# Causal masks of the score blocks: from an added product on TensorE to the reduction on VectorE, and finer waits around scores, V products and maxima

## The reference

```python
x = x + xattn(layernorm(x), ctx, ctx, Wq, Wk, Wv, bv, Wo, bo)
x = x + ffn(layernorm(x), fast_b, w_fc, w_proj, u, v, gate)

# xattn: 16 heads of 32
scores = einsum('bhsd,bhtd->bhst', qh, kh) * scale
mask = triu(ones((Sq, Sq), dtype=bool), k=0).at[0, 0].set(False)
scores = where(mask, -inf, scores)
probs = softmax(scores, axis=-1)
out = einsum('bhst,bhtd->bhsd', probs, vh)

# ffn: both weights rounded to -1, 0, 1 times a row's scale
h = bitlinear(x, w_fc) + gate * (x @ v.T @ fast_b.T @ u.T)
r = maximum(h, 0)
return bitlinear(r * r, w_proj)
```

## Time and profile before

| | |
|---|---|
| median of three executions | 2602.8 us |
| the profiled execution | 2611.11 us |
| its span, first to last instruction | 2609.3 us |
| attention phase, set-up and 16 batches | to about 1565 us |
| TensorE busy | 2522.3 us, 97% |
| VectorE busy | 1763.4 us, 68% |
| ScalarE busy | 1021.1 us, 39% |
| GpSimd busy | 789.4 us, 30% (all in the attention phase) |
| mean granted TensorE clock | 0.992 |

### The profile page before, as it was taken

One profiled execution on the slowest core, in us unless ns is written; L12 is line 12 of the kernel. 1 busy time (PEld: TensorE's weight loads), 2 busy tenths in 40 slices (PEclk: granted clock), 3 DMA queues, 4 the chain that ended last, 5 costly groups with the idle time before them and its releaser, 6 DMA issues. The chain is left out here.

```text
span 2609.3 us, 45260 instructions
## 1 busy us (share of the span) xinstructions
PE 2522.3 (97%) x13762; PEld 1908.1 (73%) x13762; DVE 1763.4 (68%) x3748; ACT 1021.1 (39%) x1887; POOL 789.4 (30%) x1498
## 2 busy tenths in 40 slices
PE   6999999999999999999999989999999999999998
PEld 5676677677667667667667758888888888888887
DVE  5676776776776677677677665666666666666663
ACT  3433533433433443353343344333333333333332
POOL 1743643654564473474365350000000000000000
PEclk9999999999999999999999999999999999999999
DMA  4444354354354344445435341111111111111111
GB/s 150 114 125 128 95 143 131 77 156 119 88 146 132 88 127 133 115 108 133 135 84 154 117 130 37 48 48 48 48 48 48 48 48 48 48 48 48 48 52 46
DMA packets 147811, 240.79 MB, mean 92 GB/s; under 512 B 26419, under 2 KB 34611, under 8 KB 147780
## 3 DMA queue, kind: packets, MB, share of 16 engines
q1 hardware_dynamic: 143684, 239.35, 32.1%
q10 hardware_dynamic: 4096, 1.06, 0.2%
HBM read 100.85 MB, written 37.77 MB: 53 GB/s over the span
## 5 line engine op out<-in xcount | busy, mean ns | idle before, releaser
L845 ACT ACTIVATE probs<-bank 128x512 f32<-128x512 f32 x640 | 358.4, 597 | 287.9 <-PE bank L633 278.7
L1243 PE MATMUL h_bank<-xT_hi,wT 128*128 128x512 f32 x1024 | 398.4, 389 | 0.5 <-ACT projT L1274 0.5
L1244 PE MATMUL h_bank<-xT_lo,wT 128*128 128x512 f32 x1024 | 398.3, 389 | 0.0
L1258 PE MATMUL y_bank<-projT,wT 128*128 128x512 f32 x1024 | 398.3, 389 | 0.0
L1260 PE MATMUL y_bank<-projT,wT 128*128 128x512 f32 x1024 | 398.3, 389 | 0.0
L1310 ACT ACTIVATE acc<-h_bank,scale_fc 128x512 f32<-128x512 f32 x256 | 176.4, 689 | 487.4 <-PE h_bank L1247 487.4
L532 POOL TENSOR_SCALAR_AFFINE_SELECT probs<-probs 128x256 f32<-128x256 f32 (+1 forms) x640 | 229.1, 372 | 212.0 <-ACT probs L845 204.1
L608 PE MATMUL bank<-stack 96*128 96x512 f32 (+3 forms) x1024 | 263.0, 337 | 21.5 <-DMA stack<-stage 15.1
L937 DVE CUSTOM_DVE_ANT_0 bank<-bank,masks 128x512 f32<-128x512 f32 x256 | 178.3, 696 | 141.1 <-PE bank L608 132.9
L633 PE MATMUL bank<-stack 98*128 98x512 f32 (+3 forms) x1024 | 259.1, 337 | 11.6 <-DMA stack<-m_stage 8.7
L1386 DVE CAST wT<-acc 128x512 fp32r<-128x512 f32 x256 | 108.4, 423 | 214.2 <-ACT acc L1315 214.2
(11 more groups left out here) (173 smaller groups left out, 4641.4 us busy)
## 6 DMA issues: line engine op xcount, KB each, us to landing
stack<-stage SPq DMA_DIRECT2D x768, 128.0 KB, 2.3
xc_rows<-in_x_dram SPq DMA_DIRECT2D x16, 1024.0 KB, 5.3
x_res<-in_x_dram SPq DMA_DIRECT2D x16, 1024.0 KB, 6.0
x<-x_res SPq DMA_DIRECT2D x64, 256.0 KB, 2.3
xc_rows<-x SPq DMA_DIRECT2D x16, 1024.0 KB, 5.6
x_res<-x SPq DMA_DIRECT2D x16, 1024.0 KB, 7.7
out_dram<-y_sb SPq DMA_DIRECT2D x64, 256.0 KB, 2.0
xc_rows<-in_ctx_dram SPq DMA_DIRECT2D x15, 1024.0 KB, 5.3
```

What stands on the lines that cost most here:

```text
L845: act.activation(probs[:, s[2], :], t_bank[u % 2][:, :], ACT.Exp, scale=SCALE).then_inc(exp_done, 1)
L1243: pe.matmul(h_bank[b % 2][:, :], fcT[:, k, cols], xT_hi[:, k, :], start=k == 0, stop=False)
L1244: pe.matmul(h_bank[b % 2][:, :], fcT[:, k, cols], xT_lo[:, k, :], start=False, stop=False)
L1258: pe.matmul(y_bank[j][:, :], a_hi[:, b % RING, P * j:P * j + P], projT[:, b, :], start=b == 0, stop=False)
```

## The change

- All masks are added by VectorE. The mask products of line 612 go. For units 1 and 3 VectorE issues two `tensor_tensor_reduce` of 384 and 128 columns, for unit 4 two of 256, where it had two plain reductions or one. Each is followed by its accumulator read. All units now have their wait alone in front.
- Each head has a `qk_stacked` semaphore of its own. S waits at k = 0 for the three copies of the pair's first head, at k = 2 for those of the second. ScalarE waits for all heads before it overwrites `stage`.
- PV of row block 0 waits for 8 selected units, of row block 1 for 9, of row block 2 for 10.
- SEND issues the copy of the rounded maxima behind `m_hi`, and waits for `m_free` only ahead of the second copy.

```diff
-        qk_stacked = [[sem(f"qk_stacked{s}{p}") for p in range(2)] for s in range(2)]
+        qk_stacked = [[sem(f"qk_stacked{s}{h}") for h in range(GH)] for s in range(2)]
...
+        mask_row = masks[:, :, :].rearrange("p m x -> p (m x)")
...
-                                     ).then_inc(qk_stacked[g % 2][pair], 16)
+                                     ).then_inc(qk_stacked[g % 2][h], 16)
...
                 if u < 4:
                     block(2 * pair + u // 2, 2, 384, 0)
-                    block(2 * pair + u // 2, 0, 128, 384, start=False)
-                    return mask(out[:, 256:512], masks[:, 3:5, :].rearrange("p m x -> p (m x)"))
+                    return block(2 * pair + u // 2, 0, 128, 384, start=False, stop=True)
                 block(2 * pair, 1, 256, 0)
-                block(2 * pair + 1, 1, 256, 256, start=False)
-                return mask(out[:, :].rearrange("p (h t) -> p h t", h=2)[:, :, P:2 * P],
-                            masks[:, 3:4, :].broadcast_to([P, 2, P]))
+                return block(2 * pair + 1, 1, 256, 256, start=False, stop=True)
...
-                        if s[2] in (0, 5):
-                            pe.wait_ge(qk_stacked[s[1] % 2][s[2] // 5], (i * 2 + s[1] // 2 + 1) * 96)
+                        if s[2] % 5 in (0, 2):
+                            pe.wait_ge(qk_stacked[s[1] % 2][2 * (s[2] // 5) + s[2] % 5 // 2], (i * 2 + s[1] // 2 + 1) * 48)
...
+                        if r != 3:
+                            pe.wait_ge(selected, i * TB + UNITS * g + {0: 8, 1: 9, 2: 10}[r])
                         if r == PV_ORDER[0]:
-                            pe.wait_ge(selected, i * TB + UNITS * g + UNITS)
...
-                        wait_alone(act, act_passed, (m_free, i * GROUPS + s[1] + 1))
-                        for part in range(2):
+                        for part, (written, value) in enumerate(((m_hi, i * GROUPS + s[1] + 1),
+                                                                 (m_free, i * GROUPS + s[1] + 1))):
+                            wait_alone(act, act_passed, (written, value))
                             act.dma_start(stack[s[1] % 2][96 + part:97 + part, 0, :, :].bitcast(F32)
...
-                            for p in range(2):
-                                staged(act, [q[p] for q in qk_stacked], s[1], b, 96)
+                            for h in range(GH):
+                                staged(act, [q[h] for q in qk_stacked], s[1], b, 48)
...
+                        wait_alone(dve, dve_passed, (s_full, i * SB + u + 1))
+
+                        def largest(first, behind, mask_from, col):
+                            return dve.tensor_tensor_reduce(bank_u[:, first:behind], bank_u[:, first:behind],
+                                                            mask_row[:, mask_from:mask_from + behind - first], 1.0, LOWEST,
+                                                            ALU.add, ALU.max, maxima[:, col:col + 1])
+
                         if k < 4 and k % 2 == 0:
-                            wait_alone(dve, dve_passed, (s_full, i * SB + u + 1))
-                        else:
-                            dve.wait_ge(s_full, i * SB + u + 1)
...
+                            last = largest(0, 512, 0, 4 * (2 * pair + k // 2) + 3)
                         elif k < 4:
                             col = 4 * (2 * pair + k // 2)
-                            dve.tensor_reduce(maxima[:, col + 2:col + 3], bank_u[:, 0:384], AX.X, ALU.max)
-                            last = dve.tensor_reduce(maxima[:, col:col + 1], bank_u[:, 384:512], AX.X, ALU.max)
+                            largest(0, 384, 128, col + 2)
+                            last = largest(384, 512, 512, col)
                         else:
-                            col = 8 * pair + 1
-                            last = dve.tensor_reduce(maxima[:, col:col + 5:4],
-                                                     bank_u[:, :].rearrange("p (h t) -> p h t", h=2), AX.X, ALU.max)
+                            largest(0, 256, 256, 8 * pair + 1)
+                            last = largest(256, 512, 256, 8 * pair + 5)
                         last.then_inc(s_free, 1)
```

More of the change, by code:

```diff
@@ L609, in block @@
                                      start=start, stop=stop, skip_group_check=True)
-                def mask(view, added):
-                    return pe.matmul(view, ident_bf[:, :], added, start=False, stop=True, skip_group_check=True)
                 if u < 4 and u % 2 == 0:
@@ L930, in program @@
                         pair, k = divmod(s[2], 5)
-                        if k < 4 and k % 2 == 0:
-                            wait_alone(dve, dve_passed, (s_full, i * SB + u + 1))
-                        else:
-                            dve.wait_ge(s_full, i * SB + u + 1)
-                        if k < 4 and k % 2 == 0:
-                            col = 4 * (2 * pair + k // 2)
-                            last = dve.tensor_tensor_reduce(bank_u[:, :], bank_u[:, :],
-                                                            masks[:, 0:4, :].rearrange("p m x -> p (m x)"), 1.0, LOWEST,
-                                                            ALU.add, ALU.max, maxima[:, col + 3:col + 4])
+                        wait_alone(dve, dve_passed, (s_full, i * SB + u + 1))
[3 more added lines that the diff above has]
+                                                            ALU.add, ALU.max, maxima[:, col:col + 1])
+                        if k < 4 and k % 2 == 0:
+                            last = largest(0, 512, 0, 4 * (2 * pair + k // 2) + 3)
                         elif k < 4:
                             col = 4 * (2 * pair + k // 2)
-                            dve.tensor_reduce(maxima[:, col + 2:col + 3], bank_u[:, 0:384], AX.X, ALU.max)
-                            last = dve.tensor_reduce(maxima[:, col:col + 1], bank_u[:, 384:512], AX.X, ALU.max)
-                        else:
-                            col = 8 * pair + 1
-                            last = dve.tensor_reduce(maxima[:, col:col + 5:4],
-                                                     bank_u[:, :].rearrange("p (h t) -> p h t", h=2), AX.X, ALU.max)
+                            largest(0, 384, 128, col + 2)
+                            last = largest(384, 512, 512, col)
+                        else:
+                            largest(0, 256, 256, 8 * pair + 1)
+                            last = largest(256, 512, 256, 8 * pair + 5)
                         last.then_inc(s_free, 1)
```

## The result

The changed kernel takes 2562.98 us (median of 4, 2561.48 to 2564.32) where the kernel before takes 2601.91 us (median of 4): the ratio is 0.9851, with a 95% interval of 0.9834 to 0.9869. That is 39 us less. The forecast was 62 us less, 2541 us, with a range of 2517 to 2577. The sign and the range hold; over a third of the gain is missing. Nearest to the result lie rival 3, at 2559 us, and rival 1, at 2569 us.

A forecast was written before the change was run, and what follows sets the result against it. TensorE, busy 97%, was taken as the bound. Per batch -2.9 masks, -1.3 scores of group 3, -0.45 in group 3, +0.8 VectorE make -3.85 us, times 16 = -62 us: 2541 us, range 2517 to 2577.

The forecast's parts named there:

- rival 3: A stretch of TensorE at the lower clock comes in every batch, 18 us lost: 2559 us; chance 0.09.
- rival 1: Waits return on the way from last score through ScalarE, VectorE, SP to next scores: 2569 us; chance 0.22.
- Finer waits: Shorter stalls at PV, T and scores: 1.3 us a batch at scores of group 3, 0.45 us in group 3.
- the four stretches at the lower clock: TensorE at 1.2 GHz behind stalls in four of fifteen stretches, 1.5 us each; 6 us gained if they end.
- VectorE, +0.8 us a batch, +13 us: Split maxima cost 0.1 us a unit; seven or eight units at group 3 and M of group 2 lose 0.8 us.
- Masks, -2.9 us a batch, -46 us: Removing 24 mask products a batch from TensorE, 0.12 us each, gives 2.9 us a batch, 46 us in all.
- Rival 2: VectorE saturates: paired accumulating instructions run serially, 11.6 us a batch, slower if over a third delays TensorE; 2621 us; chance 0.04.
- Reads beside their followers: On VectorE, the second of paired accumulating instructions starts within 0.05 us of what its columns ask for.
- the two stalls gone: First score unit of group 3 without a wait for `stack`; second issue of the maxima right behind VectorE's part.
- Scores every 0.23 us: On TensorE, 512 columns every 0.23 us through the score units, without mask products.
- Idle of TensorE under 2 us a batch and a batch of 90 us: Signs of the forecast: TensorE idle under 2 us a batch; 90 us a batch, where it was 94, confirms the sum.
- the last sentence of the prediction: Prediction wrong if a batch is longer than 92 us, above all if TensorE then waits for VectorE's maxima.

The follow-up runs named there:

- the single runs: Kernel before with one finer wait each: copies awaited by head 2584.25 us, rounded maxima sent ahead 2606.13 us, PV waiting by row block 2612.45 us.
- waits_alone: The change without its mask part (TensorE adds masks, VectorE's maxima as before; finer waits kept): 2572.77 us, 0.9887 of the kernel before.
- plain_maxima: The change with VectorE's old plain reductions in units 1, 3 and 4, no mask products, so masks left out there: 2549.39 us, 0.9798 of before.
- pv_only: The kernel before with only PV waiting by row block: 2612.45 us, 1.0043 of the kernel before.
- masks_alone: The kernel before with only the mask part of the change: 2599.75 us, 0.9991 of the kernel before.
- heads_pv: The kernel before with copies awaited head by head and PV waiting by row block, maxima still sent together: 2586.26 us, 0.9947 of before.

## Why the prediction was right, and where its size was off

**Finer waits, -28 us: right.** Measured -29.5. The places were right: in the change PV, T of group 2 and the scores of group 3 follow without a wait. The steps were costed together, as one series, and the single runs show why this matters. Left out of the sum were the four stretches at the lower clock, and rightly so: the profiled execution had a mean clock of 0.992, the 41 others of the kernel before that ran beside the experiments 0.992 to 0.997 and 0.994 on average, and the four of waits_alone 0.995. Little of the lower clock was in the medians.

**VectorE, +0.8 us a batch, +13 us: right in size, with some luck.** The instructions cost 0.09 us a unit more on average, predicted 0.1, and 13.6 us came of it. The prediction put this on the seven or eight units of group 3 and M of group 2. Start by start against plain_maxima (mean of 13 batches), TensorE of the change comes later by 0.33 us at M of group 2, 0.27 and 0.16 at two score units of group 3 and 0.43 at M of group 3, which is 1.2 us there and not 0.8. Another 1 us comes at score units of groups 0 to 2. About as much comes back, since the sums of group 2 wait 0.5 us less and the transposes behind T of group 2 0.4 us less. Up to M of group 2 VectorE takes back all that the masks give: M starts 46.9 us behind the last addition to `x_res` in waits_alone, 46.1 in plain_maxima and 47.1 in the change (47.7 before; means of twelve batches), although 18 masks of the batch lie on the way.

**Masks, -2.9 us a batch, -46 us: the step that failed.** With VectorE's old form they are worth 23.4 us, 1.5 us a batch. Two things were wrong. The first is the price of a mask. The prediction took 0.96 us for two score units, two masks and one more product and subtracted three loads of 512 columns of 0.235 us. The same stretch in the change has no mask:

```profile
1064.23 0.69 PE L609 MATMUL bank<-stack 96*128 96x384 f32 x4
...
1065.00 0.40 PE L600 MATMUL bank<-cT_lo,wT 128*128 128x512 f32 x1
```

It takes 0.77 us and not 0.71: a score unit in two pieces takes longer than one load of 512 columns. Two masks in succession cost 0.19 us, and a single one, in plain_maxima against waits_alone, 0.07 to 0.12 us. With four such pairs and 16 single ones a batch that is about 2.2 us a batch, 35 us in all (an estimate), not 46. The second is the path. The prediction said that TensorE stands on it nearly throughout, so that removing 24 products gives 2.9 us "where no other wait takes their place", and then priced no such wait. A busy share of 97% hides that many of TensorE's starts come just in time for a bank, for the layer norm's queue on VectorE or for GpSimd's sums. Start by start, plain_maxima hands back against waits_alone 0.3 us at the sums of group 2, 0.1 at those of group 1, 0.2 at a score unit of group 1 and a T unit behind it, and 0.5 us in four of 13 batches at a score unit of group 2: some 0.8 us a batch on average. The transposes' wait gets 0.25 us shorter. Price and waits together leave about 1.7 us a batch where 1.5 was measured; the rest is spread over small steps and stays open.

**Rivals.** Rival 3, the lower clock in every batch, came nearest in time, 4 us off, by luck: in the change no batch but the first has such a stretch. pv_only shows that its mechanism is real: one part of the change alone brings it about in most batches. Rival 1, 6 us off, named the effect (waits take the freed time), but with the wrong cause, and its sum was wrong twice: it kept the masks at 2.1 us a batch with VectorE's cost and gave the finer waits nothing, where the runs show 0.6 us and 1.8 us. It put the wait into the way from the last scores over SP to the next ones. That is right for masks_alone (0.79 to 1.29 us) and not for the change, whose stall there is gone. Rival 2, VectorE saturated, did not come: the second of a pair starts where its columns ask for, and in the trace of the change 0.14 us are never added. (Its threshold was misworked: 4.65 of 11.6 us is 40%, not a third.) "The Read-Write Bubble" of the Trainium skill ("Advanced Engine Details and Errata") says that latency is exposed between instructions. The rows agree in kind and give the size here: a unit costs 0.05 us more for units 1 and 3 and 0.17 us more for unit 4, where one reduction became two. That is 2.2 us of VectorE's time a batch, of which 13.6 us in all reached the kernel's time, and not a reason against the change.

**Points named ahead.** Reads beside their followers, the two stalls gone: so it is. Scores every 0.23 us: not quite, a unit in two pieces takes 0.25 us or more. Idle of TensorE under 2 us a batch and a batch of 90 us: 2.6 us on average of 96 and 91.7 us, just under the 92 us at which the prediction called itself wrong. So the sum was too high, and TensorE's waits for VectorE's maxima are there, as the last sentence of the prediction had it.

## What to carry to other kernels

Work that is taken off the busiest engine is worth its time only up to the next wait behind it; count for each place the slack of the engine that gives its buffers back, rather than multiplying by the engine's busy share (here half of 46 us came through). Price an instruction against the same stretch without it, not against a neighbour of another shape. Of stalls in a series the last is worth its time alone (here 16.5 us); those ahead of it bring nothing until it is gone, and may even cost time where the clock falls. A maximum that only keeps an exponential in range needs no exact mask, as long as no masked score lies so far above the others that their exponentials vanish, and the cheapest form of the step was to leave it out.

## What the runs showed of the hardware that had not been expected

A shift of idle time can lower the clock: in pv_only TensorE was idle for 0.85 and 0.80 us within two microseconds (the kernel before has 0.35 and 0.79 us at the same place), and in 9 of 14 batches the clock fell to 1.2 GHz right behind, with a mean of 0.71 in the stretch shown. The kernel was 11.7 us slower for an edit that only removes a wait. With the second of the two gaps gone (heads_pv) the clock fell in none. The Trainium skill, "TensorE: Matmul & The Clock Gate", section "HAM oscillation — how this bites in real kernels", ties such falls to idle gaps of TensorE that last several microseconds. The rows agree in kind and not in size: the falls of pv_only stand behind gaps of under 1 us each.

Not to be seen in the rows before, and only assumed by the prediction: the read of VectorE's accumulator (0.14 us in each row) starts together with the next instruction even where that one accumulates too, as the rows of the change show (1070.66, 1071.29 above), so two add-and-maximum instructions in succession do not wait for each other's reads.
